# Attention with the values stationary: turned probabilities of two tiles move, scaled by their row sum before the turn

## Chip, core and metric

The kernel runs on one core of a Trainium2 chip. The metric is the device time of one execution in microseconds. Three runs of the kernel before gave 1409.47, 1413.25 and 1413.27 us, median 1413.25. Engines in the profile: PE is TensorE's matmuls, PEld its weight loads, DVE VectorE, ACT ScalarE, POOL GpSimd, SP the engine that issues most DMAs.

## What is computed

Eight images of 256 channels and 32x32 pixels go through a conv layer L0 and an attention layer L1, each behind a group norm and added to its input. The change touches the attention, cut to its core here (n, m are the 1024 pixels, c, d the 256 channels):

```
x = x + L0_conv(_gn(x), ...)      # 1x1 convs, pools, depthwise taps, gate
x = x + L1_conv(_gn(x), w1, w2)

# L1_conv
f = x.reshape(b, c, h * w).transpose(0, 2, 1)
q = einsum('bnc,dc->bnd', f, w1)
attn = softmax(einsum('bnd,bmd->bnm', q, f) * c ** -0.5, axis=-1)
v = einsum('bnc,dc->bnd', f, w2)
mixed = einsum('bnm,bmd->bnd', attn, v)
return mixed.transpose(0, 2, 1).reshape(b, c, h, w)
```

## The kernel before

Phases A and B (the stem and the pooled levels) are not touched. Phase C runs `step` nine times: step i does the conv part of image i and the attention part of image i - 1. Step 0 has no attention, step 8 only attention, and step 7 has no chain of pooled levels (`chained`) for a next image. Every engine has its own program, written out by hand in the order in which it runs; the engines meet at semaphores (`wait`, `then_inc`), and a waiting instruction holds everything behind it on its engine.

The attention of an image works on 8 tiles of 128 rows (pixels n). For each tile t:

- `score(t)` on PE: 12 matmuls of 512 columns into a 128x1024 PSUM slot. Every product is split into high and low fp32r parts, three matmuls for one.
- `maximum(t)` on DVE: the row maximum.
- `exponent(t)` on ACT: exp into `prob`, one buffer (named `pooled` in the profile), and the row sum. It waits until the turn of tile t - 1 has read `prob`.
- `turn(t)` on PE: eight 128x128 transposes of `prob` into a PSUM slot.
- `turned_hi(t)` on ACT and `turned_lo(t)` on DVE: the high and the low part of the turned tile, into `pt_all`.
- `mix(t)` on PE: 24 matmuls of 256 columns; the turned tile is stationary, the values `v_all` move; result 128 pixels x 256 channels in `ps_o`.
- `invert(t)` on DVE: the reciprocal of the row sum. `scale_mixed(t)` on ACT: `ps_o` times it, into `mixed`.
- `turn_back(t)` on PE: two transposes of `mixed` into `ps_ot`; `add_attention(t)` on DVE adds it to the image `x1`.

Within the loop PE's order for tile t is score(t+1), turn_back(t-2), mix(t-1), turn(t). Between these stand depthwise taps of the conv part: `centre_tap` on ACT and `outer_taps`, two instructions a time, on DVE (the lines L1459 in the profile), and one step of the running maximum of the pooled levels a tile on DVE. After the loop PE goes on with `c1`, a 1x1 conv (`product_split`, L1140).

Three PSUM slots of 128x1024 are handed round (`claim`): a use waits until the third use before it has been read, so that score 3 waits for the exponent of tile 2 where `chained` holds.

Of the kernel before, what the change touches and what calls it, by code (L numbers as in the profile page):

```python
# [30 lines left out]
P = 128  # L31
B = 8
C = 256
# [836 lines left out]
TILES = N // P  # L870
BEFORE = KT * STAGES - TILES
# [7 lines left out]
def phase_c(nc, x, out, keep, levels, box, chain, pooled):  # L879

    with ExitStack() as ctx:
# [16 lines left out]
        pt_all = sb("pt_all", [P, KT, N], F32R)  # L898
# [6 lines left out]
        mixed = sb("mixed", [P, 2, C])  # L905
# [7 lines left out]
        mv = sb("c_mv", [P, CT, 2])  # L913
        gmean = sb("gmean", [P, CT])
        dev = sb("c_dev", [P, CT])
        spread = sb("c_spread", [P, CT])
        rstd = sb("c_rstd", [P, CT])
        shift = sb("c_shift", [P, CT])
# [37 lines left out]
        pv = signal("pv", TILES)  # L956
        inverse = signal("inverse", TILES)
        mixed_done = signal("mixed", TILES)
        back = signal("back", TILES)
        result = signal("result", TILES)  # L960
# [67 lines left out]
        def _(sp):  # L1028
# [3 lines left out]
            def step(i, conv, attn, chained):  # L1032
# [6 lines left out]
                if attn:  # L1039
                    wait(sp, result, i - 1, TILES)  # L1040
                    sp.dma_start(out_v[i - 1], x1[:, :, :]).then_inc(stored.sem, 16)
                    wait(sp, stored, i - 1, 16)
# [21 lines left out]
        def _(pe):  # L1064
# [8 lines left out]
            def step(i, conv, attn, chained):  # L1073
# [116 lines left out]
                def turn(t):  # L1190
                    wait(pe, prob_done, i - 1, t + 1)
# [5 lines left out]
                def mix(t):  # L1197
                    wait(pe, pt_lo_done, i - 1, t + 1)
                    wait(pe, qv_lo, i - 1, 4)
                    if t:  # L1200
                        wait(pe, mixed_done, i - 1, t)
                    split_product(ps_o[:, 0:C], [(pt_hi[:, t % 2, cols(m)], pt_lo[:, t % 2, cols(m)], v_hi[:, m], v_lo[:, m])
                                                 for m in range(N // P)]).then_inc(pv.sem, 1)

                def turn_back(t):
                    wait(pe, mixed_done, i - 1, t + 1)
                    if t:
                        wait(pe, result, i - 1, t)
                    for d in range(CT):
                        last = nc.tensor.transpose(ps_ot[:, cols(d)], mixed[:, t % 2, cols(d)], keep["ident"][:, :])  # L1210
                    last.then_inc(back.sem, 1)
# [491 lines left out]
```

## Time and profile before

| | |
|---|---|
| median of three runs | 1413.25 us |
| the profiled execution, its time | 1411.98 us |
| its span | 1410.2 us |
| PE, DVE, ACT busy | 91%, 81%, 50% of the span |
| granted clock over the span | 0.96 |
| chain of work that ended last | PE 53%, issue 13%, DVE 11%, ACT 4% |

The span is the time from the first to the last recorded instruction of that execution; its time as a run is 1.8 us longer. A group or a timeline row names the line of the kernel, the engine, the operation and its output and inputs. A wait behind a row, in square brackets, is idle time of the engine just before it and the instruction that ended it.

### The profile page before, as it was taken

Reading aid. Unit: us, or ns where it says so; the run is one execution under the profiler, and the core shown is the slowest. Engines: PE = TensorE matmul, PEld = TensorE weight load, DVE = VectorE, ACT = ScalarE, POOL = GpSimd, SP = SyncE. Lnnn points to the kernel's source line nnn. Section 1 sums busy time; section 2 is a strip of 40 time slices with the busy share of each in tenths; the row PEclk is TensorE's granted clock in tenths of the full one; section 3 lists DMA queues with packets and bytes.
Section 4 is the critical chain, followed back from the end, with each engine's and each line's share of the span. In section 5 each row is a group of like instructions: output and inputs, shape, how many; then the busy total and the mean of one; then the engine's idle time right before and its main releaser. Section 6 shows DMA issues by size and latency. Waiting matters only on the chain.

```text
span 1410.2 us, 18374 instructions
## 1 busy us (share of the span) xinstructions
PE 1278.9 (91%) x7162; PEld 1067.5 (76%) x7162; DVE 1149.0 (81%) x1217; ACT 704.2 (50%) x762; POOL 159.5 (11%) x76
## 2 busy tenths in 40 slices
PE   3569899859999999999999999999999999999697
PEld 1249898647689868986898689868986888688597
DVE  7779897898898879887998799879887988785443
ACT  0246768554465356535653654365436553654342
POOL 1557668200000000000000000000000000000000
PEclk9779999879999999999999999999999999999899
DMA  7302213110000200020002000200020002001000
GB/s 295 149 30 81 85 75 118 62 60 30 15 1 16 90 15 0 15 89 15 0 15 89 15 0 15 89 15 0 15 89 15 0 30 75 0 1 60 0 1 30
DMA packets 19319, 63.37 MB, mean 45 GB/s; under 512 B 1616, under 2 KB 4304, under 8 KB 19280
## 3 DMA queue, kind: packets, MB, share of 16 engines
q1 hardware_dynamic: 18576, 62.53, 11.9%
q8 instruction: 27, 0.44, 0.1%
q10 hardware_dynamic: 704, 0.30, 0.1%
q14 instruction: 12, 0.10, 0.0%
HBM read 37.13 MB, written 25.17 MB: 44 GB/s over the span
## 4 chain that ended last, share of the span: by engine, by line
PE 53%; issue 13%; DVE 11%; ACT 4%; DVEq 0%; ACTq 0%; POOLq 0%; POOL 0%
PE slot L1140 19%; PE slot L1178 13%; PE ps_level L1178 9%; DVE between L1459 4%; PE slot L1194 3%; PE slot L553 3%; PE slot L1118 2%; DVE a L1459 2%; PE slot L1165 1%; PE ps_level L1210 1%; ACT f_all L1329 1%; PE slot L1097 1%; ACT a L1362 1%; ACT f_all L1365 1%; DVE f_all L1486 1%
## 5 line engine op out<-in xcount | busy, mean ns | idle before, releaser
L1178 PE MATMUL slot<-f_all,q_all 128*128 128x512 f32 x768 | 197.1, 409 | 13.4 <-ACT pooled L1319 13.4
L1178 PE MATMUL ps_level<-v_all,pt_all 128*128 128x256 f32 x1536 | 200.0, 287 | 5.4 <-ACT mixed L1338 5.2
L1178 PEld LDWEIGHTS ps_level<-v_all,pt_all 128*128 128x128 f32 x1536 | 189.6, 192 | 7.7 <-DVE pt_all L1463 6.2
L1178 PEld LDWEIGHTS slot<-f_all,q_all 128*128 128x128 f32 x768 | 145.2, 195 | 44.0 <-ACT pooled L1319 14.8
L1459 DVE SCALAR_TENSOR_TENSOR a<-between,k_columns,a 128x992 f32<-128x992 f32 (+1 forms) x128 | 157.5, 1231 | 4.9 <-ACT a L1310 2.6
L1059 POOL TENSOR_TENSOR c_rstd<-c_spread,k_minus_half 128x2 f32<-128x2 f32 x8 | 5.6, 698 | 1065.9 <-DVE gmean L1531 1065.9
L1463 DVE TENSOR_TENSOR pt_all<-slot,pt_all 128x1024 fp32r<-128x1024 f32 x64 | 78.2, 1221 | 48.2 <-ACT pt_all L1324 48.2
L1118 PE MATMUL slot<-wide,k_cv 128*128 128x512 f32 x256 | 114.3, 597 | 0.0
L1333 ACT CAST v_all<-y 128x1024 fp32r<-128x1024 f32 x32 | 33.7, 1053 | 159.5 <-DVE y L1490 159.4
L1338 ACT ACTIVATE mixed<-ps_level,row_inv 128x256 f32<-128x256 f32 x64 | 30.2, 471 | 152.6 <-PE ps_level L1178 152.6
L1310 ACT ACTIVATE a<-between,k_columns 128x1024 f32<-128x1024 f32 x64 | 79.5, 1242 | 50.1 <-DVE between L1459 49.2
L1468 DVE TENSOR_REDUCE c_minus_max<-slot 128x1 f32<-128x1024 f32 x64 | 78.1, 1220 | 11.4 <-PE slot L1178 11.4
L1118 PEld LDWEIGHTS slot<-wide,k_cv 128*128 128x128 f32 x256 | 47.5, 190 | 51.4 <-issue 50.7
L1324 ACT CAST pt_all<-slot 128x1024 fp32r<-128x1024 f32 x64 | 64.9, 1014 | 38.1 <-PE slot L1194 37.9
L1319 ACT ACTIVATE pooled<-slot,c_minus_max 128x1024 f32<-128x1024 f32 x64 | 71.6, 1119 | 21.6 <-DVE c_minus_max L1468 21.6
L1459 DVE SCALAR_TENSOR_TENSOR between<-y,k_columns,between 128x992 f32<-128x992 f32 x64 | 79.4, 1250 | 1.1
L1303 ACT ACTIVATE y<-slot,k_columns 128x1024 f32<-128x1024 f32 x32 | 35.3, 1104 | 86.6 <-PE slot L1140 86.6
L1459 DVE SCALAR_TENSOR_TENSOR between<-a,k_columns,between 128x960 f32<-128x960 f32 x64 | 77.2, 1215 | 1.1
L1194 PE MATMUL slot<-k_ident,pooled 128*128 128x128 f32 x512 | 67.6, 276 | 4.0 <-ACT pooled L1319 4.0
L1490 DVE SCALAR_TENSOR_TENSOR y<-slot,k_columns,y 128x1024 f32<-128x1024 f32 x32 | 40.8, 1280 | 36.4 <-PE slot L1140 34.5
L742 POOL TENSOR_TENSOR e_lo<-x_all,e_hi 128x1024 fp32r<-128x1024 f32 x24 | 61.5, 2562 | 47.6 <-ACT e_hi L697 47.6
L1140 PE MATMUL slot<-f_all,k_c_hi 128*128 128x512 f32 x232 | 64.0, 397 | 0.0
(179 smaller groups left out, 2730.4 us busy)
## 6 DMA issues: line engine op xcount, KB each, us to landing
levels<-x_all SPq DMA_DIRECT2D x32, 512.0 KB, 2.6
x_all<-in_x SPq DMA_DIRECT2D x8, 1024.0 KB, 13.3
q_all<-levels SPq DMA_DIRECT2D x8, 1024.0 KB, 4.9
x<-in_x SPq DMA_DIRECT2D x8, 1024.0 KB, 4.8
out<-x SPq DMA_DIRECT2D x8, 1024.0 KB, 3.9
pooled<-levels SPq DMA_DIRECT2D x8, 512.0 KB, 3.4
wide<-levels SPq DMA_DIRECT2D x7, 512.0 KB, 3.3
x_all<-in_w_c SPq DMA_DIRECT2D x2, 512.0 KB, 3.9
```

Of the source, the lines that this page charges most:

```text
L553: last = nc.tensor.matmul(out[:, r0 * W:r1 * W], part[:, k * P:(k + 1) * P], box[:, c0:c0 + (r1 - r0) * W], start=(b not in started), stop ...
L742: nc.gpsimd.tensor_tensor(e_lo[:, u], e[u], e_hi[:, u].bitcast(F32), ALU.subtract).then_inc(e_lo_done, 1)
L1118: last = nc.tensor.matmul(slot[:, h * HALF:(h + 1) * HALF], keep["cv1"][:, k, cols(m)], rows, start=(k == 0), stop=(k == KT - 1))
L1140: last = nc.tensor.matmul(slot[:, hs], weights[:, k], inputs(k)[:, hs], start=(at == 0), stop=(at == len(uses) - 1))
L1178: last = nc.tensor.matmul(out, lhs, rhs, start=(n == 0), stop=(n == len(parts) - 1))
L1194: last = nc.tensor.transpose(slot[:, cols(m)], prob[:, cols(m)], keep["ident"][:, :])
L1310: nc.scalar.activation(dst, src, ACT.Identity, scale=keep["taps"][:, s, c, 1:2], bias=keep["b_taps"][:, s, c:c + 1]).then_inc(taps_centre. ...
L1319: nc.scalar.activation(prob[:, :], slots_of["s", t][:, :], ACT.Exp, bias=minus_max[:, t:t + 1], accum_out=row_sum[:, t:t + 1]).then_inc(pr ...
L1324: nc.scalar.copy(pt_hi[:, t % 2], slots_of["t", t][:, :]).then_inc(pt_hi_done.sem, 1)
L1459: nc.vector.scalar_tensor_tensor(o, u, keep["taps"][:, s, c, tap:tap + 1], o, ALU.mult, ALU.add).then_inc(taps.sem, 1)
L1463: nc.vector.tensor_tensor(pt_lo[:, t % 2], slots_of["t", t][:, :], pt_hi[:, t % 2].bitcast(F32), ALU.subtract).then_inc(pt_lo_done.sem, 1)
L1468: nc.vector.tensor_reduce(minus_max[:, t:t + 1], slots_of["s", t][:, :], AX, ALU.max, negate=True).then_inc(maxed.sem, 1)
```

## The change

The mix is turned round. The values are stationary, a 128 pixel x 128 channel block at a time, and the turned probabilities of two tiles, 256 columns, move past them. The result comes out as channels x pixels, the layout of the image, for a pair of tiles, and is added to it without a turn. `mix` now runs per half of a pair: half h makes the channels h % 2 of pair h // 2, and both halves need both tiles. Since pixels n are now columns of the result, the reciprocal row sum can no longer be a scale per partition there; `weigh(t)` multiplies `prob` with it before the turn. Pairs take `ps_o` and `ps_ot` by turns. Buffers: `pt_all` is twice as large, `mixed` is gone, `first_level` lies in `a`, `row_inv` in `row_sum`, six small tiles lie in one.

```diff
-        pt_all = sb("pt_all", [P, KT, N], F32R)
+        pt_all = sb("pt_all", [P, 2, KT, N], F32R)
...
-        pt_hi, pt_lo = pt_all[:, 0:2], pt_all[:, 2:4]
-        a_hi, a_lo, y_hi, y_lo = f_all, q_all, v_all, pt_all
+        pt_hi, pt_lo = (pt_all[:, k].rearrange("p (u k) n -> p u (k n)", u=2).rearrange("p u (m c) -> p u m c", c=C) for k in range(2))
+        a_hi, a_lo, y_hi, y_lo = f_all, q_all, v_all, pt_all[:, 0]
...
-        first_level = sb("first_level", [P, N])
+        first_level = a[:, 1]
...
-        row_inv = sb("row_inv", [P, TILES])
+        row_inv = row_sum
...
                 def turn(t):
-                    wait(pe, prob_done, i - 1, t + 1)
+                    wait(pe, weighted, i - 1, t + 1)
...
-                def mix(t):
-                    wait(pe, pt_lo_done, i - 1, t + 1)
+                def mix(half):
+
+                    pair, d = divmod(half, 2)
+                    wait(pe, pt_lo_done, i - 1, 2 * pair + 2)
                     wait(pe, qv_lo, i - 1, 4)
-                    if t:
-                        wait(pe, mixed_done, i - 1, t)
-                    split_product(ps_o[:, 0:C], [(pt_hi[:, t % 2, cols(m)], pt_lo[:, t % 2, cols(m)], v_hi[:, m], v_lo[:, m])
-                                                 for m in range(N // P)]).then_inc(pv.sem, 1)
-
-                def turn_back(t):
...
+                    if d == 0 and pair > 1:
+                        wait(pe, result, i - 1, pair - 1)
+                    own = (ps_o, ps_ot)[pair % 2]
+                    last = split_product(own[:, d * C:(d + 1) * C],
+                                         [(v_hi[:, m, cols(d)], v_lo[:, m, cols(d)], pt_hi[:, pair % 2, m], pt_lo[:, pair % 2, m])
+                                          for m in range(N // P)])
+                    if d:
+                        last.then_inc(pv.sem, 1)
...
                         if t > 1:
-                            turn_back(t - 2)
-                        if t and t + 1 < TILES:
-                            mix(t - 1)
+                            mix(t - 2)
                         turn(t)
...
-                    for t in range(TILES - 2, TILES):
-                        mix(t)
-                    turn_back(TILES - 2)
-                    if not conv:
-                        turn_back(TILES - 1)
+                    for half in range(TILES - 2, TILES):
+                        mix(half)
...
-                def scale_mixed(t):
-                    wait(act, pv, i - 1, t + 1)
+                def weigh(t):
                     wait(act, inverse, i - 1, t + 1)
-                    nc.scalar.activation(mixed[:, t % 2], ps_o[:, 0:C], ACT.Copy, scale=row_inv[:, t:t + 1]).then_inc(mixed_done.sem, 1)
+                    nc.scalar.activation(prob[:, :], prob[:, :], ACT.Copy, scale=row_inv[:, t:t + 1]).then_inc(weighted.sem, 1)
...
                     for t in range(TILES):
-                        if t > 1:
-                            scale_mixed(t - 2)
                         if t:
                             turned_hi(t - 1)
                         if t == 1 and conv:
                             centre_tap(BEFORE + 1)
                         exponent(t)
+                        weigh(t)
...
-                def add_attention(t):
-                    wait(dve, back, i - 1, t + 1)
-                    part = x1[:, :, t * P:(t + 1) * P]
-                    nc.vector.tensor_tensor(part, ps_ot[:, 0:C].rearrange("p (d n) -> p d n", d=CT), part, ALU.add).then_inc(result.sem, 1)
+                def add_attention(pair):
+                    wait(dve, pv, i - 1, pair + 1)
...
                     maximum(0)
                     if conv:
                         outer_taps(BEFORE - 1)
+                    invert(0)
                     for t in range(TILES):
                         if t:
                             turned_lo(t - 1)
+                            invert(t)
...
-                        invert(t)
-                        if t > 1:
-                            add_attention(t - 2)
+                        if t > 3 and t % 2 == 0:
+                            add_attention(t // 2 - 2)
```

What that does to the order of PE's instructions at the start of an image's loop, in steps 1 to 6. The names: `f_all,q_all` are scores, `k_ident,pooled` turns, `v_all,pt_all` mixes, `k_ident,mixed` turns back, `k_ident,wide` a turn for the pooled levels. Before, from score 1:

```order
L1178 MATMUL slot<-f_all,q_all 128x512 x12
L87 ISA
L87 REGISTER_ALU
L1194 MATMUL slot<-k_ident,pooled 128x128 x8
L1178 MATMUL slot<-f_all,q_all 128x512 x12
L1178 MATMUL ps_level<-v_all,pt_all 128x256 x24
L87 REGISTER_ALU
L1194 MATMUL slot<-k_ident,pooled 128x128 x8
L87 ISA
L1097 MATMUL slot<-k_ident,wide 128x128 x8
L87 REGISTER_ALU
L1178 MATMUL slot<-f_all,q_all 128x512 x12
```

Now, from the same score 1:

```order
L1174 MATMUL slot<-f_all,q_all 128x512 x12
L87 ISA
L87 REGISTER_ALU
L1190 MATMUL slot<-k_ident,pooled 128x128 x8
L1174 MATMUL slot<-f_all,q_all 128x512 x12
L87 REGISTER_ALU
L1190 MATMUL slot<-k_ident,pooled 128x128 x8
L87 ISA
L1093 MATMUL slot<-k_ident,wide 128x128 x8
L87 REGISTER_ALU
L1174 MATMUL slot<-f_all,q_all 128x512 x12
L1174 MATMUL ps_level<-pt_all,v_all 128x256 x24
```

The first mix has moved from between score 2 and turn 1 to behind score 3.

The end of the loop on PE, before, from the last matmul of the box sum (`box,zt_lo`) to the first rows of c1 (`k_c_hi`):

```order
L553 MATMUL slot<-box,zt_lo 128x192
L1210 MATMUL ps_level<-k_ident,mixed 128x128 x2
L87 REGISTER_ALU
L1194 MATMUL slot<-k_ident,pooled 128x128 x8
L1178 MATMUL ps_level<-v_all,pt_all 128x256 x48
L1210 MATMUL ps_level<-k_ident,mixed 128x128 x2
L1140 MATMUL slot<-f_all,k_c_hi 128x512 x6
```

And now:

```order
L553 MATMUL slot<-box,zt_lo 128x192
L1174 MATMUL ps_level<-pt_all,v_all 128x256 x24
L87 REGISTER_ALU
L1190 MATMUL slot<-k_ident,pooled 128x128 x8
L1174 MATMUL ps_level<-pt_all,v_all 128x256 x48
L1136 MATMUL slot<-f_all,k_c_hi 128x512 x6
```

A mix stands before the last turn now, where a turn back stood; behind it are two mixes as before, but both wait for the last turned tile.

DVE at the start of the loop, before, from the maximum of tile 0 (`c_minus_max`); `a<-between` and `between<-y` are taps, `pt_all` is `turned_lo`:

```order
L1468 TENSOR_REDUCE c_minus_max<-slot 128x1
L87 REGISTER_ALU
L1459 SCALAR_TENSOR_TENSOR a<-between,k_columns,a 128x960
L87 REGISTER_ALU
L1459 SCALAR_TENSOR_TENSOR a<-between,k_columns,a 128x960
L87 REGISTER_ALU
L1468 TENSOR_REDUCE c_minus_max<-slot 128x1
L1472 RECIPROCAL row_inv<-row_sum 128x1
L1463 TENSOR_TENSOR pt_all<-slot,pt_all 128x1024
L87 REGISTER_ALU
L1459 SCALAR_TENSOR_TENSOR between<-y,k_columns,between 128x32x31
```

And now:

```order
L1452 TENSOR_REDUCE c_minus_max<-slot 128x1
L87 REGISTER_ALU
L1442 SCALAR_TENSOR_TENSOR a<-between,k_columns,a 128x960
L87 REGISTER_ALU
L1442 SCALAR_TENSOR_TENSOR a<-between,k_columns,a 128x960
L1456 RECIPROCAL row_sum<-row_sum 128x1
L87 REGISTER_ALU
L1452 TENSOR_REDUCE c_minus_max<-slot 128x1
L1448 TENSOR_TENSOR pt_all<-slot,pt_all 128x8x128
L1456 RECIPROCAL row_sum<-row_sum 128x1
L87 REGISTER_ALU
L1442 SCALAR_TENSOR_TENSOR between<-y,k_columns,between 128x32x31
```

The reciprocal of tile 0 stands behind the first pair of taps, and that of tile 1 has come ahead of the next four.

## Rows read from the trace of the kernel before

**Rows 1.** The page, busy time of the engines and their instructions.

```profile
PE 1278.9 (91%) x7162; PEld 1067.5 (76%) x7162; DVE 1149.0 (81%) x1217; ACT 704.2 (50%) x762; POOL 159.5 (11%) x76
```

**Rows 2.** Windows of two attention loops (columns: length, busy of each engine, clock, DMA).

```profile
672.90:734.00 61.10, 58.21 (x405) 53.28 (x403) 57.74 (x63) 35.05 (x45) 0.00 (x0) 1.00 0.02 9
811.80:873.10 61.30, 58.41 (x392) 53.06 (x391) 56.85 (x62) 34.23 (x44) 0.00 (x0) 0.97 0.03 9
```

**Rows 3.** Windows, the stretch of score 3 in the loop at 812 us.

```profile
828.10:832.50 4.40, 4.40 (x12) 3.48 (x13) 3.54 (x4) 1.99 (x2) 0.00 (x0) 0.61 0.00 0
```

**Rows 4.** Timeline of PE, same loop (start, length, then the instruction; idle before it).

```profile
817.38 1.09 PE L1194 MATMUL slot<-k_ident,pooled 128*128 128x128 f32 x8
...
821.09 3.04 PE L1178 MATMUL ps_level<-v_all,pt_all 128*128 128x256 f32 x24
...
828.10 4.60 PE L1178 MATMUL slot<-f_all,q_all 128*128 128x512 f32 x12 [2.23 <-ACT pooled L1319]
...
836.42 3.00 PE L1178 MATMUL slot<-f_all,q_all 128*128 128x512 f32 x12
839.27 0.39 PE L1210 MATMUL ps_level<-k_ident,mixed 128*128 128x128 f32 x2
839.41 3.11 PE L1178 MATMUL ps_level<-v_all,pt_all 128*128 128x256 f32 x24
842.36 1.04 PE L1194 MATMUL slot<-k_ident,pooled 128*128 128x128 f32 x8
```

**Rows 5.** Timeline of ACT, same loop.

```profile
818.50 1.01 ACT L1324 CAST pt_all<-slot 128x1024 fp32r<-128x1024 f32 x1 [1.25 <-PE slot L1194]
...
820.56 1.10 ACT L1319 ACTIVATE pooled<-slot,c_minus_max 128x1024 f32<-128x1024 f32 x1
...
826.84 1.11 ACT L1319 ACTIVATE pooled<-slot,c_minus_max 128x1024 f32<-128x1024 f32 x1 [0.80 <-DVE c_minus_max L1468]
```

**Rows 6.** Timeline of DVE, same loop.

```profile
815.93 2.46 DVE L1459 SCALAR_TENSOR_TENSOR a<-between,k_columns,a 128x960 f32<-128x960 f32 x2
...
819.44 0.15 DVE L1472 RECIPROCAL row_inv<-row_sum 128x1 f32<-128x1 f32 x1
819.55 1.22 DVE L1463 TENSOR_TENSOR pt_all<-slot,pt_all 128x1024 fp32r<-128x1024 f32 x1
820.69 4.98 DVE L1459 SCALAR_TENSOR_TENSOR between<-y,k_columns,between 128x992 f32<-128x992 f32 x4
825.59 1.22 DVE L1468 TENSOR_REDUCE c_minus_max<-slot 128x1 f32<-128x1024 f32 x1
```

**Rows 7.** Timeline of PE, end of the same loop.

```profile
862.56 1.03 PE L1194 MATMUL slot<-k_ident,pooled 128*128 128x128 f32 x8
863.35 1.36 PE L553 MATMUL slot<-box,zt_hi 128*128 128x192 f32 x10
...
865.70 0.38 PE L1210 MATMUL ps_level<-k_ident,mixed 128*128 128x128 f32 x2
...
870.49 3.10 PE L1178 MATMUL ps_level<-v_all,pt_all 128*128 128x256 f32 x24 [0.66 <-ACT mixed L1338]
...
873.57 1.63 PE L1140 MATMUL slot<-f_all,k_c_hi 128*128 128x512 f32 x6
```

**Rows 8.** Groups by line (busy, mean ns of one, idle before it and its releaser).

```profile
L1178 PE MATMUL ps_level<-v_all,pt_all 128*128 128x256 f32 x1536 | 200.0, 287 | 5.4 <-ACT mixed L1338 5.2
...
L1310 ACT ACTIVATE a<-between,k_columns 128x1024 f32<-128x1024 f32 x64 | 79.5, 1242 | 50.1 <-DVE between L1459 49.2
...
L1338 ACT ACTIVATE mixed<-ps_level,row_inv 128x256 f32<-128x256 f32 x64 | 30.2, 471 | 152.6 <-PE ps_level L1178 152.6
...
L712 ACT ACTIVATE x_all<-x_all 128x1024 f32<-128x1024 f32 x24 | 25.4, 1059 | 0.8
```

**Rows 9.** Timeline of PE, last transposes of the seventh loop.

```profile
1279.82 1.09 PE L1194 MATMUL slot<-k_ident,pooled 128*128 128x128 f32 x8 [1.99 <-ACT pooled L1319]
```

**Rows 10.** Timeline of PE, last transposes of the eighth loop.

```profile
1394.89 1.90 PE L1194 MATMUL slot<-k_ident,pooled 128*128 128x128 f32 x8 [1.99 <-ACT pooled L1319]
```

More of the change, by code:

```diff
@@ L870 @@
 TILES = N // P
+PAIRS = TILES // 2
 BEFORE = KT * STAGES - TILES
@@ L901, in phase_c @@
         v_hi, v_lo = (v_all[:, k:k + CT].rearrange("p t (m c) -> p (t m) c", c=C) for k in (0, CT))
-        pt_hi, pt_lo = pt_all[:, 0:2], pt_all[:, 2:4]
-        a_hi, a_lo, y_hi, y_lo = f_all, q_all, v_all, pt_all
+        pt_hi, pt_lo = (pt_all[:, k].rearrange("p (u k) n -> p u (k n)", u=2).rearrange("p u (m c) -> p u m c", c=C) for k in range(2))
+        a_hi, a_lo, y_hi, y_lo = f_all, q_all, v_all, pt_all[:, 0]
         prob = pooled.second
-        mixed = sb("mixed", [P, 2, C])
         between = sb("between", [P, 2, N])
         zt_hi, zt_lo = sb("zt_hi", [P, N], F32R), sb("zt_lo", [P, N], F32R)
-        first_level = sb("first_level", [P, N])
+        first_level = a[:, 1]
         minus_max = sb("c_minus_max", [P, TILES])
         row_sum = sb("row_sum", [P, TILES])
-        row_inv = sb("row_inv", [P, TILES])
+        row_inv = row_sum
         stats = sb("c_stats", [P, CT, 2, 6])
[L913 to L918, printed above, removed]
+        small = sb("c_small", [P, 7 * CT])
+        mv = small[:, 0:2 * CT].rearrange("p (t k) -> p t k", k=2)
+        gmean, dev, spread, rstd, shift = (small[:, k * CT:(k + 1) * CT] for k in range(2, 7))
         slots = [ctx.enter_context(nc.psum_tensor(f"slot{n}", [P, N], F32)) for n in range(3)]
@@ L955, in phase_c @@
         pt_lo_done = signal("pt_lo", TILES)
-        pv = signal("pv", TILES)
+        pv = signal("pv", PAIRS)
         inverse = signal("inverse", TILES)
-        mixed_done = signal("mixed", TILES)
-        back = signal("back", TILES)
-        result = signal("result", TILES)
+        weighted = signal("weighted", TILES)
+        result = signal("result", PAIRS)
         stats_gate = ctx.enter_context(nc.semaphore("c_gate"))
@@ L1039, in step @@
                 if attn:
-                    wait(sp, result, i - 1, TILES)
+                    wait(sp, result, i - 1, PAIRS)
                     sp.dma_start(out_v[i - 1], x1[:, :, :]).then_inc(stored.sem, 16)
@@ L1280, in step @@
                         if attn and m == 0:
-                            turn_back(TILES - 1)
                             if chained:
@@ L1323, in turned_hi @@
                     wait(act, turned, i - 1, t + 1)
-                    nc.scalar.copy(pt_hi[:, t % 2], slots_of["t", t][:, :]).then_inc(pt_hi_done.sem, 1)
+                    slot = slots_of["t", t][:, :].rearrange("p (m n) -> p m n", n=P)
+                    nc.scalar.copy(pt_hi[:, t // 2 % 2, :, t % 2 * P:(t % 2 + 1) * P], slot).then_inc(pt_hi_done.sem, 1)
                 def inputs_hi(n):
@@ L1400, in step @@
                     if conv:
-                        inputs_hi(0)
-                        inputs_hi(1)
-                    scale_mixed(TILES - 2)
-                    if conv:
-                        inputs_hi(2)
-                    scale_mixed(TILES - 1)
+                        for n in range(KT - 1):
+                            inputs_hi(n)
                 if conv:
@@ L1472, in invert @@
                     nc.vector.reciprocal(row_inv[:, t:t + 1], row_sum[:, t:t + 1]).then_inc(inverse.sem, 1)
-                def add_attention(t):
-                    wait(dve, back, i - 1, t + 1)
-                    part = x1[:, :, t * P:(t + 1) * P]
-                    nc.vector.tensor_tensor(part, ps_ot[:, 0:C].rearrange("p (d n) -> p d n", d=CT), part, ALU.add).then_inc(result.sem, 1)
+                def add_attention(pair):
+                    wait(dve, pv, i - 1, pair + 1)
+                    part = x1[:, :, pair * C:(pair + 1) * C]
+                    own = (ps_o, ps_ot)[pair % 2]
+                    nc.vector.tensor_tensor(part, own[:, :].rearrange("p (d n) -> p d n", d=CT), part, ALU.add).then_inc(result.sem, 1)
                 def inputs_lo(n):
@@ L1590, in step @@
                 if attn:
-                    add_attention(TILES - 2)
+                    add_attention(PAIRS - 2)
                 if chained and not attn:
@@ L1620, in step @@
                     if attn:
-                        add_attention(TILES - 1)
+                        add_attention(PAIRS - 1)
                     if chained:
@@ L1685 @@
     nc = bacc.Bacc("TRN2", target_bir_lowering=False, num_devices=1,
-                   dynamic_dma_scratch_size=8192)
+                   dynamic_dma_scratch_size=4096)
     arrays = {"x": np.ascontiguousarray(inputs["x"]), "columns": columns(inputs)}
```

11 lines of the change are left out of this document (3 added, 8 removed).

## The prediction

> **What bounds the kernel now.** I read the page first: PE is busy for 1278.9 of 1410.2 us and DVE for 1149.0, ACT for half [rows 1]. So ACT has room for more work, and PE hardly any. A share over the whole span does not say which wait ends last, so I read the windows of the attention loops next. Each takes about 61 us, PE busy for 58.4 of 61.3 and DVE for 56.9 [rows 2]: both queues are nearly full there, and what matters is who stands behind whom in them. The timeline of one loop shows it. In a settled tile PE never waits: score 2.85 us (836.42 to 839.27), turn back 0.14, mix 2.95, turn 0.79, together 6.73 [rows 4, 7]. At the two ends it waits. At the start DVE stands behind four taps (820.69, 4.98 us), so the maximum of tile 2 starts at 825.59 only, the exponent at 826.84, and score 3 at 828.10 after 2.23 us of idle PE [rows 4 to 6]. At the end mix 7 waits 0.66 us for the scaled result of mix 6 [rows 7]. All seven loops that run beside a conv stage have this order of instructions.
>
> **What goes and what comes.** Gone on PE: 8 turn backs per image of two transposes, 0.14 us each in a settled tile (839.27 to 839.41) and 0.22 at 865.70: 9 us over 64 tiles. The mix keeps its 24 matmuls of 256 columns and 24 weight loads per half, so 2.95 us stay. Gone on ACT: 64 scalings of 0.471 us [rows 8], nobody's bound. New on ACT: 64 scalings of 128x1024 from SBUF into SBUF with one pointer operand. No row has that form. With no pointer it is 1.059 us, with two 1.242 us [rows 8]; I take the middle, 1.15, and both ends for the range. The Trainium skill ("Perfetto Trace Analysis", Optimizing Scalar/DVE Operations) puts ScalarE's access overhead on SBUF at about 93 ns and says a profiled duration shows about twice that; an estimate from it is 0.19 + 0.85 = 1.04 us, below the lowest of the two rows, and the sum by it would be under 1 us lower. The copy and the subtraction that split the turned tile now write eight runs of 128 elements. DVE's taps of 31-element rows show nothing extra (4.98 us for four, against 1.22 for 1024 plain elements) [rows 6], so I cost that at nothing; the bound above is in the rivals. The four larger additions, renamed small tiles and the halved scratch lie on no path that PE waits for.
>
> **The start of a loop.** The scaling now stands between the exponent and the turn, and behind a reciprocal. Tile 0's reciprocal is queued on DVE after the tap pair that starts at 815.93 and takes 2.46 us [rows 6]. So: 818.4, reciprocal 0.15, scaling 1.15, hand-overs 0.05 each: turn 0 starts at about 819.75 instead of 817.38, +2.4. The copy starts 1.12 after it and the exponent of tile 1 2.06 after that [rows 5], so that exponent moves from 820.56 to 822.95. Its sum is there 1.26 later (826.84 to 828.10 is that hop for tile 2): 824.2. DVE has split tile 0 by then (it needs 1.22 us from about 821.9) and stands still before the reciprocal of tile 1 with four taps behind it. Reciprocal 0.11 (819.44 to 819.55): the taps start at 824.3 instead of 820.69, +3.6. The maximum, the exponent of tile 2 and score 3 follow at fixed distances: score 3 at 831.7 instead of 828.10, **+3.6**. PE meanwhile waits 2.4 us before turn 0 and some 2 before turn 1, because mix 0 (821.09) no longer fills that gap: it needs both tiles of a pair, and comes behind score 3. From there PE does what it did, less one turn back: turn 2 is 3.5 late.
>
> **A settled tile.** From turn t-1's start to weighted tile t: copy starts at 1.12, exponent 0.9 later, sum 1.26 later, reciprocal 0.15, scaling 1.15, hops 0.1: 4.7 us. PE comes to turn t after 0.79 + 2.85 + 2.95 = 6.6 us. The scaling is hidden with 1.9 us in hand, and the reciprocal, behind the subtraction (ends at 1.12 + 1.05 + 1.22 = 3.4), costs nothing. DVE's queue, 1.14 + 0.11 + 2.45 + two of 1.14 and an addition in every second tile, is about 6.4: it just fits. Each of tiles 3 to 6 gains 0.14: **-0.6**.
>
> **The end of a loop.** Before, turn 6 starts at 862.56 and c1 at 873.57, 11.0 us, and the last turn back lies inside c1 (0.2). Now, from turn 6: turn 0.79, box sum 2.35 (863.35 to 865.70), mix 5 2.95, turn 7 0.80; then mix 6 needs the split tile 7, which comes 1.12 + 1.05 + 1.22 = 3.4 after turn 7's start, a wait of 2.6; then two mixes, 5.9: 15.4. That is **+4.2** [rows 6, 7]. Before, mix 6 covered that split.
>
> **The sum.** 3.5 - 0.6 + 4.2 = 7.1 per image in six images. In the seventh there is no box sum: start 3.6, tiles -0.6; at the end turn 7 already waited 1.99 us for its exponent [rows 9], mix 5 now fills that, but the scaling makes PE wait again by about 0.9, and the split wait is the same: about +6 in all. In the eighth no taps stand before the reciprocal, mix 5 fills the same idle time, and the last turn back and its hand-overs go: between -1.5 and +1.5, I take 0. So 6 x 7.1 + 6 = 48.6 us without the clock.
>
> **The clock.** After the 2.23 us of idle PE, score 3 takes 4.60 us instead of 3.00: granted clock 0.61 in that stretch, part of it at 1.2 instead of 2.4 GHz, 1.6 us lost [rows 3, 4]. Of the six loops with this wait one, at 673 us, kept its clock at 1.00; the other five are at 0.97 as the one at 812 us is [rows 2]. Of the two loops with 1.99 us of idle time before turn 7 one shows transposes of 1.09 and the other of 1.90 us [rows 9, 10]. So a wait of 2 us or more costs up to 1.6, and did so six times in eight. The wait of 2.6 before mix 6 is new in eight loops: 8 x 1.6 x 0.75 = 9.6. Before turn 0 it delays the chain by 0.8 at most, half of it counted in 7 loops would be 3; against that, the eighth loop's penalty is already there, -2. Together +10, between -8 (the clock drops nowhere, not even where it did in five loops) and +29 (every wait pays, and score 3's longer wait pays twice).
>
> Span 1410.2 + 48.6 + 10 = 1468.8. This execution's own time was 1.8 above its span, 1411.98; the median of the runs, 1413.25, is another 1.3 above. Forecast 1471 us.
>
> **Rivals.** (a) The forecast, slower by 40 to 78 us: 0.82. (b) Faster: the ends do not matter and only the removal counts. By the groups PE waited 5.2 us for the scaled result before a mix [rows 8]; with turn backs 9 us, the kernel would take 1399. It decides if the reciprocal of tile 0 were served before the taps, and if something covered the last split; the order of DVE and PE speaks against both. The Trainium skill says the same from the other side ("Perfetto Trace Analysis", Matmuls): matmul groups should rotate through PSUM banks so that the evacuation of one overlaps the next group; the two result banks now do, and by that rule alone the time would be these 1399 us. 0.05. (c) No difference: gains of 14 us and losses of as much, if the end wait were hidden and the start shift only 2: 0.02. (d) Mild, 1418 to 1453: the shift at the start is real, but DVE, less pressed, catches part of it up: 0.05. (e) The runs of 128 double the split on DVE (1.22 to 2.4 us) or on ACT: DVE's tile becomes 7.6 us against PE's 6.6, some 1 us in 50 tiles more, with longer ends: about 1530. Nothing in the rows of broken-up taps speaks for it: 0.06.
>
> The range reaches from 1453 (48.6 - 8, with the same 3.1 on top of 1410.2) to 1491 (48.6 + 29). About 0.3% is what a measurement of this kernel can tell from no change. Faster 0.05, same 0.03, slower 0.92.
>
> **What would show it.** DVE: the reciprocal of tile 0 behind the tap pair, that of tile 1 after about 1.1 us of idle DVE, then four taps. ACT: the scaling at 1.06 to 1.25 us. PE: waits of about 2.4 before turn 0, 2 before turn 1, over 4 before score 3, 2.6 before mix 6; no wait in tiles 3 to 6, which follow each other at 6.6 us; the loop from score 0 to c1 some 7 to 9 us longer. I am wrong if mix 6 does not wait, if turn t waits in settled tiles (then the scaling is the bound, and the time is far above), or if DVE overtakes in the loop's first 20 us.

## The result, and the profile after

The changed kernel takes 1465.75 us (median of 1463.45, 1465.75 and 1467.38), the kernel before 1412.93 us on the same chip (1409.47 to 1413.27): 52.8 us more, ratio 1.0377, with a 95% interval of 1.0358 to 1.0396. A fourth execution took 1887.56 us at a granted clock of 0.65, against 0.95 in the other three, and is in none of these numbers. The profiled execution took 1463.45 us with a span of 1461.6, 51.4 more than before.

The page of the kernel after, busy time, then four of its groups (busy, mean ns of one, idle before it and its releaser); it answers to [rows 1, 8]:

```profile
PE 1279.2 (88%) x7034; PEld 1064.9 (73%) x7034; DVE 1148.5 (79%) x1185; ACT 748.3 (51%) x762; POOL 159.5 (11%) x76
...
L1174 PE MATMUL slot<-f_all,q_all 128*128 128x512 f32 x768 | 204.1, 420 | 22.0 <-ACT pooled L1307 22.0
L1174 PE MATMUL ps_level<-pt_all,v_all 128*128 128x256 f32 x1536 | 195.9, 285 | 19.4 <-DVE pt_all L1448 19.4
...
L1190 PE MATMUL slot<-k_ident,pooled 128*128 128x128 f32 x512 | 72.1, 287 | 30.6 <-ACT pooled L1326 30.6
L1326 ACT ACTIVATE pooled<-pooled,row_sum 128x1024 f32<-128x1024 f32 x64 | 73.7, 1152 | 28.9 <-DVE row_sum L1456 28.9
```

PE's busy time is the same with 128 instructions fewer, and ACT, the only engine that works longer, is busy for half the span with its 44 us more. The time went into PE's waits. The page of before has these two groups beside the mix of [rows 8]:

```profile
L1178 PE MATMUL slot<-f_all,q_all 128*128 128x512 f32 x768 | 197.1, 409 | 13.4 <-ACT pooled L1319 13.4
...
L1194 PE MATMUL slot<-k_ident,pooled 128*128 128x128 f32 x512 | 67.6, 276 | 4.0 <-ACT pooled L1319 4.0
```

So PE's idle time rose from 13.4 to 22.0 us before scores, from 5.4 to 19.4 before mixes, and from 4.0 to 30.6 before turns. Together that is 49.2 of the 51.4 us.

The timeline of PE in the first loop beside a conv stage (start, length, instruction, idle before it and who ended it) shows where they stand; it answers to [rows 4, 7], whose loop lies at 812 us:

```profile
395.18 5.63 PE L1174 MATMUL slot<-f_all,q_all 128*128 128x512 f32 x24
403.12 1.09 PE L1190 MATMUL slot<-k_ident,pooled 128*128 128x128 f32 x8 [2.31 <-ACT pooled L1326]
403.96 2.99 PE L1174 MATMUL slot<-f_all,q_all 128*128 128x512 f32 x12
408.93 1.94 PE L1190 MATMUL slot<-k_ident,pooled 128*128 128x128 f32 x8 [1.97 <-ACT pooled L1326]
410.66 1.90 PE L1093 MATMUL slot<-k_ident,wide 128*128 128x128 f32 x8
415.04 4.61 PE L1174 MATMUL slot<-f_all,q_all 128*128 128x512 f32 x12 [2.48 <-ACT pooled L1307]
419.48 3.03 PE L1174 MATMUL ps_level<-pt_all,v_all 128*128 128x256 f32 x24
...
428.83 1.04 PE L1190 MATMUL slot<-k_ident,pooled 128*128 128x128 f32 x8
...
435.36 1.04 PE L1190 MATMUL slot<-k_ident,pooled 128*128 128x128 f32 x8
...
448.39 1.03 PE L1190 MATMUL slot<-k_ident,pooled 128*128 128x128 f32 x8
...
454.43 1.03 PE L1190 MATMUL slot<-k_ident,pooled 128*128 128x128 f32 x8
457.83 6.02 PE L1174 MATMUL ps_level<-pt_all,v_all 128*128 128x256 f32 x48 [2.36 <-DVE pt_all L1448]
463.68 1.55 PE L1136 MATMUL slot<-f_all,k_c_hi 128*128 128x512 f32 x6
```

The first row is score 0 and 1 together. Four waits stand in it, before turn 0, turn 1, score 3 and mix 6. Between turn 2 and turn 6 there is none, and the tiles follow each other every 6.52 us (428.83 to 435.36).

DVE in the same stretch, which answers to [rows 6]:

```profile
399.27 2.46 DVE L1442 SCALAR_TENSOR_TENSOR a<-between,k_columns,a 128x960 f32<-128x960 f32 x2
401.65 0.16 DVE L1456 RECIPROCAL row_sum<-row_sum 128x1 f32<-128x1 f32 x1
...
405.29 1.23 DVE L1448 TENSOR_TENSOR pt_all<-slot,pt_all 128x1024 fp32r<-128x1024 f32 x1 [2.36 <-ACT pt_all L1313]
407.53 0.16 DVE L1456 RECIPROCAL row_sum<-row_sum 128x1 f32<-128x1 f32 x1 [1.01 <-ACT pooled L1307]
407.62 4.99 DVE L1442 SCALAR_TENSOR_TENSOR between<-y,k_columns,between 128x992 f32<-128x992 f32 x4
412.53 1.22 DVE L1452 TENSOR_REDUCE c_minus_max<-slot 128x1 f32<-128x1024 f32 x1
```

Read from below: the maximum of tile 2 waits for four taps, the taps for the reciprocal of tile 1, and that for the exponent of tile 1, with DVE idle for 1.01 us in front of them. ACT, which answers to [rows 5]:

```profile
401.84 1.15 ACT L1326 ACTIVATE pooled<-pooled,row_sum 128x1024 f32<-128x1024 f32 x1 [1.25 <-DVE row_sum L1456]
...
413.78 1.11 ACT L1307 ACTIVATE pooled<-slot,c_minus_max 128x1024 f32<-128x1024 f32 x1 [1.44 <-DVE c_minus_max L1452]
```

The scaling of tile 0 starts as soon as its reciprocal is there, and turn 0 follows it (403.12).

### The profile page after: what moved, and what is told of

It reads as the page before. It is cut to its first block, busy times and chain, and to the rows that moved or that the text cites. A ratio compares the mean times of both kernels' runs of the same rounds, so it can differ in the third digit from the quotient of the medians.

```text
span 1461.6 us, 17966 instructions
## 1 busy us (share of the span) xinstructions
PE 1279.2 (88%) x7034; PEld 1064.9 (73%) x7034; DVE 1148.5 (79%) x1185; ACT 748.3 (51%) x762; POOL 159.5 (11%) x76
## 4 chain that ended last, share of the span: by engine, by line
PE 51%; issue 13%; DVE 12%; ACT 5%; DVEq 0%; POOLq 0%; ACTq 0%; POOL 0%
PE slot L1136 19%; PE ps_level L1174 11%; PE slot L1174 11%; DVE between L1442 4%; PE slot L1190 3%; PE slot L553 3%; DVE a L1442 2%; PE slot L1114 2%; PE slot L1161 1%; ACT pooled L1307 1%; DVE pt_all L1448 1%; PE slot L1093 1%; ACT pooled L1326 1%; ACT a L1350 1%; ACT pt_all L1313 1%
## 5 line engine op out<-in xcount | busy, mean ns | idle before, releaser
L1174 PE MATMUL slot<-f_all,q_all 128*128 128x512 f32 x768 | 204.1, 420 | 22.0 <-ACT pooled L1307 22.0
L1174 PE MATMUL ps_level<-pt_all,v_all 128*128 128x256 f32 x1536 | 195.9, 285 | 19.4 <-DVE pt_all L1448 19.4
L1174 PEld LDWEIGHTS ps_level<-pt_all,v_all 128*128 128x128 f32 x1536 | 192.1, 193 | 25.0 <-DVE pt_all L1448 21.7
L1174 PEld LDWEIGHTS slot<-f_all,q_all 128*128 128x128 f32 x768 | 150.9, 203 | 55.0 <-ACT pooled L1307 23.7
L1448 DVE TENSOR_TENSOR pt_all<-slot,pt_all 128x1024 fp32r<-128x1024 f32 x64 | 78.3, 1224 | 80.0 <-ACT pt_all L1313 80.0
L1313 ACT CAST pt_all<-slot 128x1024 fp32r<-128x1024 f32 x64 | 64.8, 1012 | 124.6 <-PE slot L1190 124.6
L1055 POOL TENSOR_TENSOR c_small<-c_small,k_minus_half 128x2 f32<-128x2 f32 x8 | 5.6, 698 | 1115.5 <-DVE c_small L1516 1115.5
L1190 PE MATMUL slot<-k_ident,pooled 128*128 128x128 f32 x512 | 72.1, 287 | 30.6 <-ACT pooled L1326 30.6
L1326 ACT ACTIVATE pooled<-pooled,row_sum 128x1024 f32<-128x1024 f32 x64 | 73.7, 1152 | 28.9 <-DVE row_sum L1456 28.9
L1190 PEld LDWEIGHTS slot<-k_ident,pooled 128*128 128x128 f32 x512 | 60.3, 147 | 37.7 <-ACT pooled L1326 21.4
L1114 PEld LDWEIGHTS slot<-wide,k_cv 128*128 128x128 f32 x256 | 47.5, 190 | 51.4 <-issue 50.7
```

Of the source, the lines that this page charges most:

```text
L1114: last = nc.tensor.matmul(slot[:, h * HALF:(h + 1) * HALF], keep["cv1"][:, k, cols(m)], rows, start=(k == 0), stop=(k == KT - 1))
L1174: last = nc.tensor.matmul(out, lhs, rhs, start=(n == 0), stop=(n == len(parts) - 1))
L1190: last = nc.tensor.transpose(slot[:, cols(m)], prob[:, cols(m)], keep["ident"][:, :])
L1313: nc.scalar.copy(pt_hi[:, t // 2 % 2, :, t % 2 * P:(t % 2 + 1) * P], slot).then_inc(pt_hi_done.sem, 1)
L1326: nc.scalar.activation(prob[:, :], prob[:, :], ACT.Copy, scale=row_inv[:, t:t + 1]).then_inc(weighted.sem, 1)
L1448: nc.vector.tensor_tensor(pt_lo[at], slot, pt_hi[at].bitcast(F32), ALU.subtract).then_inc(pt_lo_done.sem, 1)
```

## The experiments

They ask first what the two halves of the change cost, then which wait costs what, and then whether these waits can be moved without giving the pairs up. Times are medians of four executions where nothing else is said, and "less" is against the changed kernel's 1465.75 us. The runs were taken on several chips, on which the kernel before had medians from 1410.6 to 1412.9 us, so one or two us between two runs tell nothing.

**The pairs without the scaling.** `turn` waits for the exponent alone, `weigh` is gone, and the reciprocals stand where they did; the division by the row sum is left out.

```diff
-                    wait(pe, weighted, i - 1, t + 1)
+                    wait(pe, prob_done, i - 1, t + 1)
...
-                        weigh(t)
```

> The changed kernel without its scaling: the probabilities are turned unscaled (the division by the row sum is left out altogether), and the reciprocals stand where they stood before. What is left is the pairs alone. Theory (the ends of a loop cost, the settled tiles gain): the start no longer moves, the end still does, by about 4.1 us an image, and the five settled tiles give back 0.7: about +20 us over the kernel before, some 1432 us. Rival A (the scaling is the whole loss): 1400 to 1412 us. Rival B (the scaling is hidden and costs nothing): 1466 us as the changed kernel.

Measured: 1436.37 us, ratio 1.0168 (1.0151 to 1.0185). PE's timeline in the first loop:

```profile
405.68 1.06 PE L1190 MATMUL slot<-k_ident,pooled 128*128 128x128 f32 x8 [0.65 <-ACT pooled L1307]
...
411.88 5.27 PE L1174 MATMUL slot<-f_all,q_all 128*128 128x512 f32 x12 [4.26 <-ACT pooled L1307]
...
455.37 6.02 PE L1174 MATMUL ps_level<-pt_all,v_all 128*128 128x256 f32 x48 [2.36 <-DVE pt_all L1443]
```

The waits before turns 0 and 1 have shrunk to nothing and 0.65, so they belong to the scaling and its reciprocals, which went back with it; the one before mix 6 is unchanged, so it belongs to the pairs. Score 3 starts 16.26 us after score 0, exactly as in the kernel before. It waits 4.26, as mix 0 no longer stands ahead of it, and then takes 5.27 to 5.49 us in the six loops, where before it took 4.6 in most. That is about what the time lies above the expected 1432. The pairs alone cost 24 of the 53 us.

**The scaling without the pairs.** The kernel before, with `weigh` between exponent and turn, the reciprocals ahead as in the change, and a plain copy of `ps_o` in place of the scaled one.

```diff
+                        weigh(t)
...
-                    nc.scalar.activation(mixed[:, t % 2], ps_o[:, 0:C], ACT.Copy, scale=row_inv[:, t:t + 1]).then_inc(mixed_done.sem, 1)
+                    nc.scalar.copy(mixed[:, t % 2], ps_o[:, 0:C]).then_inc(mixed_done.sem, 1)
```

> The kernel before with the scaling alone: probabilities are scaled ahead of the turn, reciprocals placed as in the change, the result of a mix is copied unscaled and turned back as before. Theory: the start moves by 3.6 us an image in seven images, the end by 1.3 (turn 7 waits for its scaling where it stood ready), the eighth image by about 3; settled tiles move by nothing: +36 us, 1449 us, up to 8 more if the clock falls at the new wait. Rival A (the scaling is the whole loss): 1466 us. Rival B (hidden): 1413 us.

Measured: 1449.46 us, ratio 1.0262 (1.0237 to 1.0287). Turn 0 waits 2.31 us as in the changed kernel, turn 1 not at all, since mix 0 covers it, and turn 7 1.13:

```profile
402.40 1.09 PE L1195 MATMUL slot<-k_ident,pooled 128*128 128x128 f32 x8 [2.31 <-ACT pooled L1342]
...
414.32 4.61 PE L1179 MATMUL slot<-f_all,q_all 128*128 128x512 f32 x12 [3.46 <-ACT pooled L1320]
```

The scaling alone costs 37 us. The two parts apart make 1.7 + 2.6 = 4.3%, together 3.8%: they share a little of what they cost, and neither pays for the other.

**The scaling twice.** In tiles 3 to 6 a second pass over `prob` with a factor of 1.0, 32 instructions of 1.06 us.

```diff
+                    if 2 < t < TILES - 1:
+                        nc.scalar.activation(prob[:, :], prob[:, :], ACT.Copy, scale=1.0).then_inc(again.sem, 1)
+                        wait(act, again, i - 1, t - 2)
```

> The changed kernel with a second 128x1024 scaling (by one) in each of tiles 3 to 6, four a loop, 32 in all, 1.15 us each. Theory: a settled tile has 1.8 us in hand on that chain, so nothing moves: 1466 us, within 2. Rival (ACT's scaling is in the chain that sets every tile): 32 x 1.15 = 37 us more, about 1503 us.

Measured: 1465.68 us, ratio 1.0379 (1.0362 to 1.0397), no change. ACT and PE of that kernel:

```profile
431.92 1.07 ACT L1328 ACTIVATE pooled<-pooled 128x1024 f32<-128x1024 f32 x1 [0.26 <-DVE row_sum L1460]
433.02 1.16 ACT L1330 ACTIVATE pooled<-pooled,row_sum 128x1024 f32<-128x1024 f32 x1
```

```profile
434.99 1.04 PE L1191 MATMUL slot<-k_ident,pooled 128*128 128x128 f32 x8
...
441.51 1.04 PE L1191 MATMUL slot<-k_ident,pooled 128*128 128x128 f32 x8
```

The tile stays at 6.52 us. In settled tiles the scaling is hidden with over 1 us in hand; its cost lies at the ends of the loop alone.

**The reciprocal of tile 0 ahead of the taps.**

```diff
                     maximum(0)
+                    invert(0)
                     if conv:
                         outer_taps(BEFORE - 1)
-                    invert(0)
```

> The changed kernel with the reciprocal of tile 0 ahead of the pair of taps instead of behind it. Theory: turn 0 and everything behind it in the start of a loop comes 1.2 us earlier (818.55 instead of 819.75 in the prediction's example), DVE stands idle 1.2 us for it but did so later anyhow: 7 x 1.2 = 8 us less, 1458 us, perhaps a few less if the clock then no longer falls at turn 0. Rival (the start is lost by the mix that moved, not by the chain): 1466 us. Rival (DVE is full and pays for the idle time): 1466 to 1475 us.

Measured: 1462.01 us, ratio 1.0357 (1.0337 to 1.0376), 3.7 us less and not 8, and its four times (1459.27 to 1465.05) overlap with those of the changed kernel.

```profile
401.70 1.09 PE L1190 MATMUL slot<-k_ident,pooled 128*128 128x128 f32 x8 [1.29 <-ACT pooled L1326]
...
413.63 5.26 PE L1174 MATMUL slot<-f_all,q_all 128*128 128x512 f32 x12 [3.09 <-ACT pooled L1307]
...
748.16 7.51 PE L1174 MATMUL ps_level<-pt_all,v_all 128*128 128x256 f32 x48 [2.36 <-DVE pt_all L1448]
```

Turn 0 waits 1.0 us less, as wanted, and keeps its clock in all seven loops, where it had lost 3.3 us in the changed kernel. But score 3, after a wait of 3.09, takes 5.26 us, and 5.49 in the next loop, where the change had 4.61 in both: 2.6 us more over the six loops. Mix 6 and 7, still behind a wait of 2.36, now run slowly in the third, the sixth and the seventh loop (7.51, 7.36 and 8.63 us for 6.01), 5.5 us more. So in this execution more than half of what the chain gained went back to the clock.

**The four taps split.** The pair of taps that stood behind the reciprocal of tile 1 goes into the gap ahead of the split of tile 0, behind the maximum of tile 1.

```diff
-                        if conv and t == 1:
-                            outer_taps(BEFORE)
...
                         if t + 1 < TILES:
                             maximum(t + 1)
+                        if conv and not t:
+                            outer_taps(BEFORE)
```

> The changed kernel with the first of the two tap pairs of tile 1 moved into DVE's idle time before the subtraction of tile 0 (2.36 us in the trace). Theory: the four taps behind the reciprocal of tile 1 are what makes the maximum of tile 2, and so score 3, late; with two of them done in the gap score 3 comes 2.4 us earlier in six images and mix 0 in the seventh: 17 us less, 1449 us. Rival (PE's missing mix at the start is the loss, DVE only fills time): 1466 us.

Measured: 1441.51 us, ratio 1.021 (1.0192 to 1.0227): 24 us less, more than the 17 expected. DVE, then PE:

```profile
400.69 2.53 DVE L1442 SCALAR_TENSOR_TENSOR between<-y,k_columns,between 128x992 f32<-128x992 f32 x2
403.14 1.22 DVE L1448 TENSOR_TENSOR pt_all<-slot,pt_all 128x1024 fp32r<-128x1024 f32 x1
405.37 0.16 DVE L1456 RECIPROCAL row_sum<-row_sum 128x1 f32<-128x1 f32 x1 [1.00 <-ACT pooled L1307]
```

```profile
406.77 1.09 PE L1190 MATMUL slot<-k_ident,pooled 128*128 128x128 f32 x8 [1.93 <-ACT pooled L1326]
...
410.43 3.04 PE L1174 MATMUL slot<-f_all,q_all 128*128 128x512 f32 x12 [1.70 <-ACT pooled L1307]
```

DVE's idle 2.36 us before the split are filled. From turn 1 to score 3 PE now takes 3.66 us (406.77 to 410.43) against 6.11 (408.93 to 415.04). And score 3 takes 3.04 instead of 4.61: after a wait of 1.70 it runs at the full clock. In this loop that makes 2.45 + 1.57 = 4.0 us. The six images together became 21.7 us shorter and not 24, since mix 6 ran slowly in two of them (7.51 and 7.41 us); the profiled execution was also 2.2 us ahead before the first loop, which this edit does not touch.

**The box sum behind the last turn.**

```diff
-    TURN_AT, BOX_AT = 1, TILES - 2
+    TURN_AT, BOX_AT = 1, TILES - 1
```

> The changed kernel with the box sum of the pooled levels (2.35 us of PE) behind the last turn instead of behind turn 6. Theory: it covers the wait of 2.36 us for the split of the last tile; turn 7 then waits about 0.9 us for its scaling instead, so mix 6 starts some 1.6 us earlier in the six images that have a box sum: 10 us less, 1456 us. Rival (what the end lost comes back as another wait, the scaling's or the pooled levels'): 1464 to 1468 us.

Measured: 1455.79 us, ratio 1.0303 (1.0286 to 1.032), 10 us less in the median, as expected; the span of the profiled execution is 6.2 less, six images by 1.33 would be 8.

```profile
448.02 1.04 PE L1190 MATMUL slot<-k_ident,pooled 128*128 128x128 f32 x8
...
452.67 1.09 PE L1190 MATMUL slot<-k_ident,pooled 128*128 128x128 f32 x8 [0.76 <-ACT pooled L1326]
453.52 1.36 PE L553 MATMUL slot<-box,zt_hi 128*128 128x192 f32 x10
...
456.12 6.02 PE L1174 MATMUL ps_level<-pt_all,v_all 128*128 128x256 f32 x48
```

The 20 matmuls of the box sum stand in the gap before mix 6, which no longer waits. Turn 7 loses its cover and waits 0.76. From turn 6 to c1 (461.98) it is 13.96 us against 15.29.

**Both moves.** The last two edits together.

> The changed kernel with both moves, the tap pair in the gap and the box sum behind the last turn. Theory: the two places are apart, so the gains add: 27 us less, 1439 us. Rival (they share one wait): about 1449 us. Either way still slower than the kernel before at 1413 us.

Measured: 1427.58 us, ratio 1.0108 (1.0091 to 1.0125). That is 38.2 us less; the two alone gave 24.2 and 10.0, so they add up, and a little more. Most of the 11 us by which it beats the estimate is what the clock gave back at score 3: it takes 3.01 to 3.04 us in all six loops, where it took at least 4.4.

**And the reciprocal of tile 0 between the two taps of its pair.** With six executions.

```diff
                     if conv:
-                        outer_taps(BEFORE - 1)
+                        outer_taps(BEFORE - 1, (0,))
                     invert(0)
+                    if conv:
+                        outer_taps(BEFORE - 1, (1,))
```

> The version with the tap pair in the gap and the box sum behind the last turn, and on top the reciprocal of tile 0 between the two instructions of the tap pair ahead of it, so that DVE neither delays it by a pair nor stands idle for it. Theory: turn 0 comes 1.2 us earlier and with it the exponent of tile 1, its reciprocal and, through the maximum of tile 2, score 3: 7 x 1.2 = 8 us less, 1419 us. Rival (it only moves the waiting from turn 0 to turn 1 or score 3): 1427 us.

Measured: 1422.16 us, ratio 1.0078 (1.0059 to 1.0096), 5.4 us less than the version before it and not 8. Turn 0 waits 1.29 us instead of 2.31, and turn 1 2.02 and score 3 1.66 as before, so the wait was taken away and not moved. DVE of that kernel shows the reciprocal start 1.35 us after the first tap, where it had to wait 2.38:

```profile
397.72 1.21 DVE L1444 SCALAR_TENSOR_TENSOR a<-between,k_columns,a 128x960 f32<-128x960 f32 x1
399.07 0.16 DVE L1458 RECIPROCAL row_sum<-row_sum 128x1 f32<-128x1 f32 x1
```

**The pooled level turned in a result bank.** The slot that score 3 waits for is the third use back. The turn of the pooled level (`wide`) goes into `ps_level`, which is free until mix 0, so that score 3 has its slot one use earlier. With 12 executions.

```diff
+            plan["zt", 0] = ps_level
...
+                    if half == 0 and chained:
+                        wait(pe, chain.lo_done, i, 1)
```

> As the run before, and the turn of pooled level 0 goes into the result banks, which are free until mix 0, instead of into a slot; score 3 then takes the slot of tile 0 and no longer waits for the exponent of tile 2. The split of the level moves ahead on ACT and DVE, its first maxima back, and mix 0 waits for that split. Theory: the wait of some 1.3 to 1.7 us before score 3 goes, and turn 2 follows from the chain of tile 2 alone, 2 us earlier in six images: 12 us less than the run before, 1407 us, which would be under the kernel before at 1412. Rival (DVE is full there, so mix 0 or turn 2 waits by as much): 1417 to 1420 us.

Measured: 1415.22 us, ratio 1.0031 (1.0018 to 1.0044), 7 us less than the run before and 8 us above the expectation. The wait before score 3 is gone, but the clock is not back. PE in the second loop:

```profile
545.87 1.09 PE L1192 MATMUL slot<-k_ident,pooled 128*128 128x128 f32 x8 [2.03 <-ACT pooled L1330]
546.79 1.67 PE L1095 MATMUL ps_level<-k_ident,wide 128*128 128x128 f32 x8
548.11 4.10 PE L1176 MATMUL slot<-f_all,q_all 128*128 128x512 f32 x12
```

The slow stretch has moved to the wait of 2.03 before turn 1: the pooled turn takes 1.67 instead of 1.04, score 3 4.10 instead of 3.02. So it is in five of the six loops (score 3 from 3.16 to 4.20 us).

**The pooled level turned ahead of turn 1.** It fills part of that gap; its split on ACT and DVE moves with it. With 12 executions.

```diff
-                        turn(t)
                         if chained and t == TURN_AT:
                             turn_level(0)
+                        turn(t)
```

> As the run before, with the turn of pooled level 0 ahead of turn 1, in PE's wait of 2.0 us for the scaled tile 1, and its split on ACT and DVE ahead of that of tile 1. Theory: score 3 follows turn 1 at once, mix 0 then waits some 0.9 us for the split of tile 1, and turn 2 comes 1.5 us earlier in six images: 9 us less than 1415, 1406 us; where the clock fell at turn 1 it may give a little more. That is under the kernel before (1411) by some 0.3%. Rival (the wait for the split of tile 1 takes all of it back): 1413 to 1415 us.

Measured: 1409.71 us against 1411.91 of the kernel before (16 executions), ratio 0.9981 (0.9969 to 0.9993). PE:

```profile
404.81 1.03 PE L1095 MATMUL ps_level<-k_ident,wide 128*128 128x128 f32 x8
407.00 1.09 PE L1192 MATMUL slot<-k_ident,pooled 128*128 128x128 f32 x8 [1.15 <-ACT pooled L1330]
407.85 3.02 PE L1176 MATMUL slot<-f_all,q_all 128*128 128x512 f32 x12
411.73 3.13 PE L1176 MATMUL ps_level<-pt_all,v_all 128*128 128x256 f32 x24 [0.85 <-DVE pt_all L1454]
```

With no wait over 1.3 us in the first 35 us of this loop the score keeps 3.02. This is the only version with pairs that is not behind the kernel before, by 0.2%, less than the 0.3% that I called telling: the same time, reached with five moves.

It does not show that pairs gain anything. In the profiled executions each of the six images takes 138.1 us here. In the kernel before five of them take 139.6, and the third, whose score 3 kept its clock, 138.0. So what this version wins in the six images is as much as the kernel before loses at score 3, and the seventh image still takes 4.4 us more. No run gave the kernel before the same moves, such as the pooled turn out of the way of score 3: whether it would then be the faster one is open.

## Why the prediction was right

The forecast was 1471 us, and the likeliest case (a) came true, 5 us lower. By its own steps:

- **The start, +3.6: right.** From the first score to score 3 it is 19.86 us now (395.18 to 415.04). Before, the loop in the same place had 16.26, so score 3 comes 3.60 later. The waits in this loop were 2.31 before turn 0 (2.4 forecast), 1.97 before turn 1 (2), 1.01 of idle DVE (1.1). The taps behind it took 4.99. The split of those taps, the edit aimed at this chain, gave 24 us.
- **Before score 3, "over 4": right in four loops of six** (4.14 and 4.15), against 2.48 and 2.91 in the other two, where turn 1 and the pooled turn ran slowly and used up part of the same wait. The start of score 3 is the same by either.
- **The scaling, 1.15 us: right** (1.152 mean of 64), and hidden in settled tiles, which the doubled scaling shows. The Trainium skill's overhead ("Perfetto Trace Analysis", Optimizing Scalar/DVE Operations) gave an estimate of 1.04: here the trace does not agree, by 0.11 us. It agrees within 0.02 with the row that has no pointer operand, 1.059.
- **A settled tile, -0.14: a little more**, 6.52 instead of 6.73 [rows 4, 7], -0.21, since the mix after a turn back took 3.11 and now takes 3.04.
- **The end, +4.2: right.** From turn 6 to c1 it is 15.29 (15.4 forecast) against 11.0 [rows 7]; the wait before mix 6 is 2.36 (2.6) in all eight loops.
- **The strided writes at nothing: right.** `turned_hi` takes 1012 ns with eight runs of 128 elements, 1.01 us before [rows 5], `turned_lo` 1224 ns against 1.22 us [rows 6]. Rival (e) falls.
- **The sum without the clock: somewhat too high.** The first image, whose turn 0 kept its clock, lasts 146.02 us from its first matmul (383.86 to 529.88), against 139.57 before with score 3 equally slow in both: +6.45 where 7.1 was forecast. The difference is mostly in the tiles: from score 3 to turn 6 it is 33.35 us against 34.48 before, 1.1 less where 0.7 was forecast. The seventh step costs 5.3 (6).
- **The clock, +10: mis-sized, about 6.** The term that was wrong is the largest of this sum. The step of the prediction that failed is "So a wait of 2 us or more costs up to 1.6, and did so six times in eight", applied to mix 6 at 9.6 us. In seven loops mix 6 and 7 took 6.01 to 6.02 us after the 2.36 of idle time, at the full clock. The eighth alone shows the loss, 1.5 us in place of 9.6. Rows of PE's timeline at the end of the seventh and the eighth loop:

```profile
1332.02 6.01 PE L1174 MATMUL ps_level<-pt_all,v_all 128*128 128x256 f32 x48 [2.36 <-DVE pt_all L1448]
...
1449.02 7.49 PE L1174 MATMUL ps_level<-pt_all,v_all 128*128 128x256 f32 x48 [2.36 <-DVE pt_all L1448]
```

- The clock fell at the start of the loop instead. Turn 0 ran slowly in four of seven loops (1.74 to 1.97 us for 1.09), each time with turn 1 later by as much, together 3.3 us, as the 3 forecast. Score 3 is slow in all six loops, up to 5.22, where one of six had kept its clock before: 2.3 us more. With 0.7 net in the eighth step this makes 6.3. That the total came within 4 us of the forecast is luck in part: the term for mix 6 was 8 us too high, and the 2.3 at score 3 stood only in the upper bound.
- The seven loops without a loss are not typical either. Five kernels keep this wait in the first six loops (the changed one, the two without scaling or with it twice, the reciprocal first, the taps split): there mix 6 was slow in 4 of 30 loops. In the seventh loop it was slow in nine of the ten kernels with pairs (7.37 us and more), the changed one being the exception, and in the eighth in all ten.

Of the 7.2 us by which the forecast of the span was too high (1468.8 against 1461.6), some 4 are the clock and the rest the terms above. 2 of them came back because the median lies 4.1 above the span of this profiled execution, not 3.1, and because 1471.9 had been rounded down. This execution had the highest granted clock of the three (0.953 against 0.948 twice), so in the median the clock's part is probably larger than in this sum.

The rivals: (b) is out. The 9 us of turns back are gone, and yet the time rose. The Trainium skill's rule ("Perfetto Trace Analysis", Matmuls) that matmul groups rotate through PSUM banks so that one is evacuated while the next computes is borne out as far as it goes: the 5.2 us that PE waited before mixes for the evacuation (`ACT mixed` [rows 8]) are gone. But the idle time before mixes rose to 19.4 us, all of it ended by `DVE pt_all`. The mix waits for its input now, not for its bank. The condition that I had put to (b), the reciprocal before the taps and something over the last split, was then built: alone these do not bring it below the time before, and the pooled level had to move as well. (c) and (d) are out by the measured 3.60 and 2.36.

What stays open: why 2.36 us of idle PE before mix 6 cost the clock in nearly every seventh and eighth loop and seldom in the six before them. The last two have less work on PE around them, but no run varied that alone. Nor did any run separate the mix's new shape from the rest at equal waits; its 24 matmuls take 3.02 to 3.06 us in 44 of 48 rows, against 3.04 to 3.12 before, so little is to be found there.

## What to carry to other kernels

When an operation moves onto a chain that repeats per tile, look at the first and the last tile and not at the settled ones: there it was hidden with over 1 us in hand and cost nothing even when doubled, while its 37 us lay at the ends. Working in pairs takes a short pipeline's cover away at both ends (mix 0 comes later, mix 6 needs the last tile), so look for independent work that can stand in these gaps, here two taps, a box sum and a pooled turn, before counting the gain. A tiny instruction in an in-order queue (a reciprocal of 0.16 us behind 2.46 us of taps) can set the path, and the place of its neighbours is the cheapest thing to change. When a reworked version has caught up with the old one, look at what the old one loses at the same place before calling it a draw.

## What was not expected of the hardware

- The same idle time does not always cost the clock. After 2.31 us before turn 0 the turn took 1.09 us in three loops and 1.74 to 1.97 in four; after 2.36 before mix 6 nothing was lost in seven loops, and 1.47 us in the eighth, while in other kernels the same wait cost 1.4 to 2.6 us in the seventh loop. A rule "so many us of idle time cost so much" held only on average, so a forecast should give this term a range.
- The number of waits does not settle it either. With one wait of 2.23 us (the kernel before) score 3 is slow in five loops of six. With 2.31, 1.97 and 1.70 us in a row, as in the two kernels with the taps split, it takes 3.01 to 3.04 in all twelve loops; what was slow in seven of them was turn 0 or turn 1, which shortened the next wait. With 1.29, 2.02 and 1.66 score 3 is slow in one of six, and with the last of these taken away, so that 1.29 and 2.02 are left, in five of six. With 1.29, 1.15 and 0.85 to 0.89 us neither a turn nor the score was slow in any of the six.
- A wait taken away can be paid back by the clock: with the reciprocal first, turn 0 came 1.0 us earlier, and score 3 took 5.26 and 5.49 us instead of 4.61, and mix 6 and 7 lost 5.5 us in three loops.
- Each pointer operand of a 128x1024 ACTIVATE on SBUF seems to take about 0.09 us: 1.06 with none, 1.152 with one, 1.24 with two. The forms differ in more than that, so it is a reading of three rows and no measurement by itself.
